# RWKV stage of a decoder on one Trainium2 core: normalisation a group ahead, exponents between the takes, one product moved from GpSimd to VectorE

## The reference, cut to what matters

```
h = _layernorm(x)
...   # k, v, r: projections of token-mixed h with Wk, Wv, Wr and biases
def step(carry, kv):
    aa, bb, pp = carry
    kt, vt = kv
    ww = bonus + kt
    p = jnp.maximum(pp, ww)
    e1 = jnp.exp(pp - p)
    e2 = jnp.exp(ww - p)
    out = (e1 * aa + e2 * vt) / (e1 * bb + e2)
    ww2 = pp + decay
    p2 = jnp.maximum(ww2, kt)
    e1 = jnp.exp(ww2 - p2)
    e2 = jnp.exp(kt - p2)
    return ((e1 * aa + e2 * vt, e1 * bb + e2, p2), out)
...
x = x + (sigmoid(r) * outs) @ Wo + bo
```

## Time and profile before

| | us |
|---|---|
| median of 3 runs | 1564.72 |
| lowest to highest | 1561.58 to 1565.18 |
| profiled execution | 1564.23 |
| its span in the profile | 1562.4 |
| TensorE / VectorE / ScalarE / GpSimd busy | 1339.1 / 1063.2 / 836.4 / 604.2 |
| the first stage ends at | 155.3 |

### The profile page before, as it was taken

How to read it: one execution, slowest core, us unless ns; L and a number is a source line. 1 busy time by engine, 2 the same in 40 slices (tenths; PEclk the granted TensorE clock), 3 DMA queues, 4 the chain that set the end, 5 groups by cost and what they waited for, 6 DMA issues and landing times. The chain is left out here.

```text
span 1562.4 us, 26743 instructions
## 1 busy us (share of the span) xinstructions
PE 1339.1 (86%) x8097; PEld 1051.9 (67%) x8144; DVE 1063.2 (68%) x2062; ACT 836.4 (54%) x1853; POOL 604.2 (39%) x687
## 2 busy tenths in 40 slices
PE   5885788886999999946899899989997888888998
PEld 4663455554888888835777677767776556556887
DVE  5789788885466676668776777777775566653443
ACT  4433688885544344335566566656664355552332
POOL 2100755556530000027755665666664432320000
PEclk9897799998999999978999999999999799998999
DMA  8000333323000000011000000000000000000000
GB/s 309 1 0 13 81 82 81 81 67 135 1 1 1 1 0 0 1 50 49 1 1 0 0 0 0 0 0 0 0 1 0 6 4 3 3 1 1 14 14 27
DMA packets 30736, 40.26 MB, mean 26 GB/s; under 512 B 4368, under 2 KB 25872, under 8 KB 29264
## 3 DMA queue, kind: packets, MB, share of 16 engines
q1 hardware_dynamic: 30672, 39.45, 8.2%
HBM read 28.96 MB, written 2.10 MB: 20 GB/s over the span
## 5 line engine op out<-in xcount | busy, mean ns | idle before, releaser
L1792 ACT ACTIVATE wi_weights<-wi_psum,wi_bias,wi_scale 128x128 f32<-128x128 f32 x256 | 113.7, 454 | 113.0 <-DVE wi_bias L1902 112.9
L1567 POOL TENSOR_TENSOR wi_straight<-wi_straight,wi_crossed 128x512 f32<-128x512 f32 x80 | 109.9, 1373 | 5.8 <-DVE wi_crossed L1888 5.7
L932 DVE TENSOR_REDUCE gq_top<-gq_psum 128x4 f32<-128x512 f32 x128 | 86.6, 677 | 29.0 <-PE gq_psum L819 28.2
L1555 POOL TENSOR_TENSOR wi_scratch<-wi_sums,wi_eps 128x4 f32<-128x4 f32 x80 | 35.6, 445 | 158.9 <-DVE wi_sums L1871 157.3
L1893 DVE TENSOR_REDUCE wi_top<-wi_psum 128x4 f32<-128x512 f32 x64 | 44.0, 687 | 73.6 <-PE wi_psum L1682 73.6
L886 ACT ACTIVATE gq_weights<-gq_weights 128x512 f32<-128x512 f32 x128 | 81.1, 634 | 21.9 <-DVE gq_weights L940 20.6
L826 PE MATMUL gq_psum<-const,gq_weights 128*128 128x128 f32 x512 | 79.7, 279 | 14.9 <-ACT gq_weights_t L892 14.9
L1106 POOL TENSOR_TENSOR ex_scratch<-ex_squares,ex_eps 128x4 f32<-128x4 f32 x12 | 2.4, 200 | 232.8 <-ACT ex_junk L1217 232.8
L1230 ACT ACTIVATE ex_hidden_high<-ex_gated 128x512 fp32r<-128x512 f32 x64 | 40.4, 632 | 94.9 <-DVE ex_gated L1303 94.9
L1303 DVE TENSOR_TENSOR ex_gated<-ex_gated,ex_psum 128x512 f32<-128x512 f32 x64 | 43.9, 686 | 67.2 <-PE ex_psum L1158 56.6
L1556 POOL TENSOR_TENSOR wi_scale<-wi_scratch,minus_half 128x4 f32<-128x4 f32 x80 | 84.5, 1057 | 6.3
(11 more groups left out here) (343 smaller groups left out, 4083.4 us busy)
## 6 DMA issues: line engine op xcount, KB each, us to landing
gq_keys<-in_ctx_keys_dram SPq DMA_DIRECT2D x16, 512.0 KB, 3.8
gq_keys_diagonal<-gq_key_parts SPq DMA_DIRECT2D x64, 128.0 KB, 3.8
x<-in_x_dram SPq DMA_DIRECT2D x4, 512.0 KB, 7.5
gate<-in_gate_dram SPq DMA_DIRECT2D x2, 1024.0 KB, 5.9
up<-in_up_dram SPq DMA_DIRECT2D x2, 1024.0 KB, 7.9
down<-in_down_dram SPq DMA_DIRECT2D x2, 1024.0 KB, 9.9
wq<-in_wq_dram SPq DMA_DIRECT2D x1, 2048.0 KB, 9.5
wo<-in_wo_dram SPq DMA_DIRECT2D x1, 2048.0 KB, 13.9
```

The source lines that it names most:

```text
L932: dve.tensor_reduce(top[:, u % 4, :], rows(u), AX.X, ALU.max).then_inc(topped, 1)
L1567: added_up = pool.tensor_tensor(straight[:, at], straight[:, at], crossed[:, at], ALU.add)
L1792: act.activation(weights[:, g % 2, j, :], ps[:, SC + g % 2, j * P:j * P + P], ACT.Exp, bias=bias[:, g % 2, j:j + 1], scale=scale[:, g, j:j ...
```

## The change

The hardware loops of TensorE, ScalarE, VectorE are written out, GpSimd's products go. What moves:

- ScalarE normalises group g+1 between the takes of k and v of group g, with `turn(g)` long done, and does `weigh(g)` between the takes of v and r of the same group. `pad_h(g)` and all takes of g now stand in round g.
- VectorE makes `e2v` itself, first thing in `accumulate`. `divide(g-1)` stands ahead of `lower(g+1)`. The statistics of groups 2 and 3 are taken behind `scan(0)`; `rstd` and `shift` come in three parts.
- TensorE does bias and output of group g-1 together, behind the projection of k.
- The last group's output goes to banks 2 and 3 (`out_bank`), its bias as soon as k is out of them; `add(2)` stands behind `divide(3)`. `add` goes half by half, statistics with it.
- A wait for `out_ready` ahead of each product in `divide` keeps `rw` from being overwritten.

```diff
 (TensorE)
-            def bias(g, last):
-                if not last:
-                    pe.wait_ge(lowered, KC * (g + 3))
-                need(pe, added, GB * g)
+            def bias(g):
+                if g == NG - 1:
+                    pe.wait_ge(taken, 3 * KC * g + KC)
+                else:
+                    pe.wait_ge(lowered, KC * min(g + 3, NG))
+                    need(pe, added, GB * g)
...
-                    bias(g - 1, last)
+                    bias(g - 1)
+                    output(g - 1)
                 if not last:
                     project(g + 1, 1)
-                if not first:
-                    output(g - 1)
-                if not last:
                     project(g + 1, 2)
 (ScalarE)
-            for m in range(3):
-                take(0, m)
+            take(0, 0)
             act.wait_ge(shift_ready, 2)
-            def one(g, first, last):
-                if not last:
+            normalise(1)
+            take(0, 1)
+            weigh(0)
+            take(0, 2)
+            own.again()
+            def one(g):
+                pad_h(g)
+                take(g, 0)
+                if g + 1 < NG:
+                    act.wait_ge(shift_ready, 3)
                     normalise(g + 1)
-                    pad_h(g + 1)
+                take(g, 1)
                 weigh(g)
-                if not last:
-                    for m in range(3):
-                        take(g + 1, m)
+                take(g, 2)
                 own.again()
 (VectorE)
                     own.wait()
+                    need(dve, out_ready, 2 * g - 1 + i)
                     dve.tensor_tensor(by_pair(rw, i), by_pair(num, i), by_pair(den, i),
...
             def accumulate(g):
+                dve.wait_ge(weight, 3 * g + 1)
+                dve.wait_ge(taken, 3 * KC * g + 2 * KC)
+                dve.tensor_tensor(tokens(e2v), tokens(e2), tokens(v), ALU.mult).then_inc(e2v_ready, 1)
                 dve.wait_ge(weight, 3 * g + 2)
...
             def one(g, first, last):
                 scan(g)
+                if first:
+                    for later in range(2, NG):
+                        statistics(later)
+                    dve.wait_ge(rstd_ready, 3)
+                    find_shift(2 * GB, NB)
+                else:
+                    divide(g - 1)
                 if not last:
                     lower(g + 1)
-                if not first:
-                    divide(g - 1)
                 accumulate(g)
-                if not first:
+                if not first and not last:
                     add(g - 1)
                 own.again()
-            rounds(dve, one)
+            for g in range(NG):
+                one(g, g == 0, g == NG - 1)
             divide(NG - 1)
+            add(NG - 2)
             add(NG - 1)
```

More of the change, by code:

```diff
@@ L294, in by_pair, with out_bank @@
             return tile[:, :, 2 * P * i:2 * P * i + 2 * P]
+        def out_bank(g):
+            return 2 if g == NG - 1 else 0
         def col(base, c):
@@ L309, in _ @@
             pool.memset(net.ones[:], 1.0).then_inc(preset, 1)
-            def one(g, first, last):
[L312 to L316, removed]
+            for first, end in ((GB, 2 * GB), (2 * GB, NB)):
+                scale_of(pool, own, net, scratch, aggregated, rstd_ready, first, end)
             pool.wait_ge(net.keys_in, 16)
@@ L319, in _ @@
             split_keys(pool, Own(pool, net.own_keys), net)
-            rounds(pool, one)
         @block.tensor
@@ L367, in output @@
                     for c in range(KC):
[L368 removed]
+                        mm = pe.matmul(ps[:, out_bank(g) + j // 2, (j % 2) * D:(j % 2) * D + D],
+                                       rw[:, c, j * P:j * P + P],
                                        net.rwkv_w[:, 3, c, :], start=False, stop=(j % 2 == 1 and c == KC - 1))
@@ L395, in _ @@
                 project(0, m)
-            rounds(pe, one)
-            bias(NG - 1, True)
+            for g in range(NG):
+                one(g, g == 0, g == NG - 1)
+            bias(NG - 1)
             output(NG - 1)
@@ L466, in _ @@
             act.wait_ge(decay_exp, 2)
-            for m in range(3):
-                take(0, m)
+            take(0, 0)
             act.wait_ge(shift_ready, 2)
-            def one(g, first, last):
-                if not last:
+            normalise(1)
[8 more added lines that the diff above has]
+                    act.wait_ge(shift_ready, 3)
                     normalise(g + 1)
-                    pad_h(g + 1)
+                take(g, 1)
                 weigh(g)
-                if not last:
-                    for m in range(3):
-                        take(g + 1, m)
+                take(g, 2)
                 own.again()
-            rounds(act, one)
+            for g in range(1, NG):
+                one(g)
             act.wait_ge(projected, 3 * KC * NG)
@@ L541, in add @@
             def add(g):
[L542 to L549, removed]
+                for i in range(2):
+                    dve.wait_ge(out_ready, 2 * g + i + 1)
+                    for j in (2 * i, 2 * i + 1):
+                        b = GB * g + j
+                        dve.tensor_tensor(net.x[:, b, :], net.x[:, b, :],
+                                          ps[:, out_bank(g) + i, (j % 2) * D:(j % 2) * D + D],
+                                          ALU.add).then_inc(added, 1)
+                    for j in (2 * i, 2 * i + 1):
+                        dve.wait_ge(added, GB * g + j + 1)
+                        dve.bn_stats(net.stats[:, GB * g + j, :], net.x[:, GB * g + j, :])
             def statistics(g):
@@ L593, in _ @@
             split_w(1)
+            statistics(1)
             split_w(2)
-            for g in range(1, NG):
-                statistics(g)
             dve.wait_ge(rstd_ready, 2)
-            find_shift(GB, NB)
+            find_shift(GB, 2 * GB)
             dve.wait_ge(shift_ready, 2)
```

2 lines of the change are left out of this document (1 added, 1 removed).

## The result

The changed kernel takes 1541.11 us (median of 4 runs, 1539.97 to 1544.03) beside 1563.15 us of the kernel before (4 runs, 1560.64 to 1565.18); ratio 0.9863, 95% interval 0.984 to 0.9885. Two later comparisons gave 0.9853 (0.9836 to 0.987) and 0.9882 (0.9853 to 0.9912), that is 23.6 and 16.5 us. The direction was forecast; the size was not: 22.0 us between the medians against some 18 forecast, and 1541.1 lies under the range's end of 1542.5.

What follows compares the result with a forecast made beforehand. TensorE's work plus its round trip over ScalarE bounded the middle passes, VectorE next. Start 7.0, middle passes 9.1 and tail 3.0 made 19.1 us, less 0.8 gave 18.3; 1564.23 became 1545.9, stated as 1546.0, range 1542.5 to 1551.

Steps and rivals of the forecast that it cites:

- charge for TensorE's clock: First stage: 0.8 us taken off VectorE's gain of 19.1 for TensorE's late output, leaving 18.3.
- TensorE's ring: Middle passes before the change: TensorE's work plus the round trip over ScalarE, said to set the period of 31.0 us.
- the collisions: VectorE's products held up by GpSimd's e2v: 1.6 us in a middle pass, 1.4 at the start, said to go.
- the tail: Last pass and tail of the first stage: add(2) fills VectorE's 1.95 us wait; 38.66 becomes 35.7, 3.0 us gained.
- the output would be there at 68.6, wanted at 71: Middle pass: TensorE's output(g-1) ready before VectorE's add(g-1) needs it, with room for some 2.3 us of clock losses.
- rival 1: TensorE sets the middle passes; VectorE waits 1.2 to 1.6 us in each pass and the last; 1548.6 us; chance 0.17.
- rival 2: e2v on VectorE takes 2.4 us instead of 1.14, or collisions stay; 4.9 us less gain, 1550.8; chance 0.07.
- rival 3: The gain does not reach the end: the next stage waits for something with a fixed time; 1564 us; chance 0.04.
- rival 4: Slower: ScalarE's pauses ahead of each projection keep TensorE at its low level; 45 us slower, 1610; chance 0.01.
- Rival 5: Better than forecast: waits downstream of the first stage shrink too; under 1544 us; chance 0.05.
- The hole ahead of the projection: TensorE's pause in a middle pass, waiting for pad_h: to shrink from 3.0 + 1.3 to 1.3 to 1.8 us.
- their start moves with it: Later stages begin with statistics of x at the first stage's end and wait for nothing else; the 18.3 us carries through.

## Why the prediction was right in the first stage and wrong in the whole

Forecast against measured, from the same profile positions:

| step | forecast | measured |
|---|---|---|
| lowering of group 1 starts | 35.8 | 35.80 |
| scan(1) starts | 47.5 | 47.37 |
| two middle passes | 53.0 | 53.04 |
| scan(3) to the end of the last statistics | 35.7 | 35.9 |
| charge for TensorE's clock | 0.8 | 0.44 |
| stage, gain | 18.3 | 19.0 |
| later stages | 0 | 3.5 less, 2.5 more in the profile |

The last statistics end 0.3 us ahead of the next stage in both kernels (155.29, 136.32). The walk along VectorE held at every join, though its first entry is to the hundredth by luck: over six profiles of the new order that lowering starts at 35.04 to 35.91. The experiments bear out the reasons: TensorE's ring, not the collisions, was the bound; division and normalisation each carry the change only with the other; the tail gives 1.6 us; e2v on VectorE takes 1.22 and moves what follows by 1.14 (37.00 to 38.14). Less well held that the output would be there at 68.6, wanted at 71: TensorE finished it at 71.97, because the projection of k took 8.3 us at the lower clock instead of 5.65, and VectorE wanted the second half of it at 72.31. That just fitted; in pass 2 it came 0.44 late. So rival 1 did begin, with 0.44 us of the 3.5 that it puts on the stage end (139.7 against 136.2).

Rivals 2, 3 and 4 did not happen. The row that rival 3 was answered from covers 40 to 60 us only (the DMA share is 0.13 from 120 to 140, the next stage's keys); the next stage takes 219.0 and 218.8 us in the two kernels, so nothing in it waited. Rival 5's time, under 1544, did come, but not by a wait that shrank behind the first stage: what was smaller was the expert stage's clock loss, 3.4 us for 6.8.

One step inside was wrong without harm. The hole ahead of the projection was to be 1.3 to 1.8 us; ahead of 58.01 it was 3.54. I counted `weigh` from the take of v, but in pass 1 ScalarE had v at 48.67 and waited for z, which VectorE gives at 50.3. TensorE had room for that.

The step that failed is "their start moves with it": that the later stages carry their length over from the profile before, a term put at nothing. That profile had an expert stage with its clock loss at the high end, 6.8 us, which is one of the values 1.7, 3.4, 5.1 and 6.8 that unchanged code takes. The sum was made against an execution and should have been made against a distribution. The same term also set the range: I took its lower end from three runs of the kernel before, 2.7 us under the profiled one, when that kernel has runs 7.3 us under it (1556.91). It was not the draw of one comparison: the changed kernel came out under the range's 1542.5 in all three comparisons (1541.11, 1540.77, 1542.29).

The second of its profiles, an execution of 1541.32 us near these medians, shows where the time lies: of the 22.9 us between its span and the first profile's, the first stage holds 18.8, the expert stage 3.6, the other four together 0.5.

What can be put down to the new order is the difference of the mean stage ends, 155.8 less 136.1, 19.7 us. Whether the change also shifts how often the expert stage loses much is open: on the first chip the kernel before was at its higher level in 28 of 29 runs, and the changed kernel's four all lie at 1540.15 to 1542.67, with 3.4 us lost in the one profiled. Where both kernels lost 6.8 us in the expert stage, the spans are 1562.4 and 1563.1 against 1541.4, 21.0 and 21.7 us; the first stage holds 20.1 and 20.7 of it in that pair.

## What to carry to other kernels

When two engines wait for each other in a ring, moving one step off the ring pays only together with work that fills the other's hole: cost both engines' chains in the new order, join by join, and the larger one is the new pass. Before a forecast rests on one profile, ask which of its stages hold a granted clock under 1.00 while TensorE is busy, and give each such piece back to the range on the side on which it can vanish. A collision between VectorE and GpSimd inside a pass that neither bounds costs nothing: removing it left the middle passes at 32.0 and 30.9 us.

## What the runs showed of the hardware

The granted clock fell also where TensorE had had no long hole. In the expert stage of the first profile it fell three times, near 462, 534 (twice as long) and 609 us, and the longest hole in the 10 us ahead of each was 0.52, 0.69 and 0.69 us. The losses come in pieces of about 1.7 us, at the same few places of the program (80, 150 to 160 and 220 to 230 us into the expert stage), in some executions and not in others. One kernel on one chip thus had two levels 7 us apart (1556.2 to 1558.8 and 1563.1 to 1567.1). The shares differed between chips: 1 of 29 executions at the low level on the first, 13 of 17 on the second, 12 of 23 on the third.

In the first stage a hole of 1.75 us left the clock up (1.18 us for four matmuls) in all six profiles of the new order. One of 3.54 was followed by 2.04 to 2.05 us in three of them and by 1.18 in the other three. The output of pass 2 lost 1.7 us in all six (5.41 for 3.72) with no hole of over 1 us in the 5 us ahead of it. A product of VectorE that fell on one of GpSimd's ended 0.55 us behind it (the one at 55.86 at 57.70, GpSimd's of 54.80 at 57.15), alone it takes 0.69; a reciprocal was not held up (3.35 us at 83.02, beside GpSimd's product of 83.29, and 3.35 without one).

The Trainium skill ("TensorE: Matmul & The Clock Gate", HAM oscillation) ties such falls to gaps in TensorE's work. The hole of 3.54 us agrees in three profiles and not in three; the stretch with TensorE busy for 19.98 of 20 us at 0.84 does not.
